# Experts' whole blocks: gate and up weights held in TensorE, turned rows streamed

## The reference, cut to what matters

```python
def _swiglu(combined):
    gate, up = jnp.split(combined, 2, axis=-1)
    return jax.nn.silu(gate) * up
...
combined = jnp.einsum('td,efd->tef', xf, expert_gate_up)   # d = 512, f = 2 * 512
hidden = _swiglu(combined)
expert_out = jnp.einsum('tef,edf->ted', hidden, expert_down)
sel_out = jnp.take_along_axis(expert_out, sel[:, :, None], axis=1)
routed_out = jnp.einsum('tk,tkd->td', gating, sel_out)
```

## Time and profile before

| | us |
|---|---|
| median of 3 runs | 1439.57 |
| lowest, highest | 1436.03, 1440.11 |
| span of the profiled execution | 1442.9 |
| TensorE busy in it | 1308.7 (91%) |
| VectorE, ScalarE, GpSimd busy | 583.3, 467.2, 200.8 |

### The profile page before, as it was taken

The page is one execution under the profiler, slowest core; times in us unless marked ns, Lnnn a source line. Parts: engine busy times, 40 slices in busy tenths (PEclk is TensorE's granted clock), DMA queues, the critical chain, the costliest instruction groups (busy, mean ns, idle before and its releaser), DMA issues.

```text
span 1442.9 us, 18224 instructions
## 1 busy us (share of the span) xinstructions
PE 1308.7 (91%) x5770; PEld 831.9 (58%) x5771; DVE 583.3 (40%) x1559; ACT 467.2 (32%) x1004; POOL 200.8 (14%) x207
## 2 busy tenths in 40 slices
PE   4899999999999899899898998988669999999798
PEld 3554485566466454377565775665445567565365
DVE  9999732111243351111111111111175333685894
ACT  5899632122122200011111111111113233227884
POOL 1000000000000055010100111101263000022370
PEclk8999999999999899999999999999879989999899
DMA  9100000000101214231246115253462000100001
GB/s 223 55 1 1 2 1 1 1 1 1 77 31 32 95 50 129 97 126 49 94 150 216 44 44 195 66 199 95 164 177 100 1 30 1 67 0 1 1 23 51
DMA packets 40976, 97.06 MB, mean 67 GB/s; under 512 B 4205, under 2 KB 6567, under 8 KB 39745
## 3 DMA queue, kind: packets, MB, share of 16 engines
q1 hardware_dynamic: 27205, 68.70, 14.3%
q0 software_dynamic: 6240, 16.39, 4.2%
q10 hardware_dynamic: 7452, 10.97, 2.1%
HBM read 79.91 MB, written 16.10 MB: 67 GB/s over the span
## 4 chain that ended last, share of the span: by engine, by line
PE 75%; DVE 11%; DMA 4%; issue 3%; ACT 3%; ACTq 1%; DVEq 1%; another core or an unknown queue 1%; POOL 0%; POOLq 0%
PE psum L433 38%; PE psum L1813 13%; PE psum L1868 7%; PE psum L1793 4%; DMA slot_outs<-sb_blk 3%; PE psum L2008 3%; PE psum L461 2%; DVE sb_hT_conv L1408 1%; PE psum L1951 1%; PE psum L1893 1%; PE psum L1925 1%; ACT sb_htok L807 1%; DMA sb_blk<-rows,sb_blk 1%; PE psum L1843 1%; DVE sb_blk L1201 1%
## 5 line engine op out<-in xcount | busy, mean ns | idle before, releaser
L433 PE MATMUL psum<-sb_w_reg,sb_blk 128*128 128x256 f32 x896 | 207.3, 385 | 1.2 <-issue 1.2
L433 PEld LDWEIGHTS psum<-sb_w_reg,sb_blk 128*128 128x128 f32 x896 | 170.1, 193 | 33.7 <-issue 12.4
L1813 PE MATMUL psum<-sb_z_reg_r,sb_hT_conv_r 125*125 125x512 f32 x400 | 170.9, 427 | 0.2 <-issue 0.2
L433 PE MATMUL psum<-sb_w_reg,sb_hT_conv 128*125 128x512 f32 (+1 forms) x376 | 168.6, 598 | 0.0
L1813 PE MATMUL psum<-sb_htok_r,sb_hT_conv_r 125*125 125x512 f32 x300 | 118.8, 396 | 0.0
L433 PE MATMUL psum<-sb_hT_conv,sb_w_reg 128*128 128x416 f32 (+3 forms) x336 | 108.2, 481 | 8.1 <-ACT sb_hT_conv L467 8.1
L1198 DVE TENSOR_TENSOR sb_blk<-sb_blk,psum 128x256 f32<-128x256 f32 x56 | 23.6, 421 | 227.4 <-ACT sb_blk L781 227.4
L433 PEld LDWEIGHTS psum<-sb_w_reg,sb_hT_conv 128*125 128x125 f32 (+1 forms) x376 | 68.6, 188 | 76.9 <-issue 76.3
L1868 PE MATMUL psum<-sb_w_reg,sb_blk 128*128 128x512 f32 x224 | 109.2, 610 | 2.2
L760 ACT CAST sb_hT_conv_r<-sb_a_reg 125x625 fp32r<-125x625 f32 x80 | 56.1, 715 | 116.6 <-PE psum L1813 116.5
L433 PEld LDWEIGHTS psum<-sb_hT_conv,sb_w_reg 128*128 128x128 f32 x336 | 67.2, 204 | 44.4 <-issue 40.3
(11 more groups left out here) (388 smaller groups left out, 1815.7 us busy)
## 6 DMA issues: line engine op xcount, KB each, us to landing
sb_hT_conv<-w_expert SPq DMA_DIRECT2D x7, 2048.0 KB, 12.5
sb_w_reg<-w_expert SPq DMA_DIRECT2D x6, 2048.0 KB, 10.6
sb_hT_conv<-w_expert SPq DMA_DIRECT2D x7, 1024.0 KB
slot_outs<-sb_blk ACTq DMA_DIRECT2D x28, 256.0 KB
sb_w_reg<-w_expert SPq DMA_DIRECT2D x6, 1024.0 KB, 12.6
sb_w_reg<-w_gnn SPq DMA_DIRECT2D x1, 4096.0 KB, 43.8
sb_w_reg<-w_qkv SPq DMA_DIRECT2D x1, 3072.0 KB, 20.5
slot_outs<-sb_blk ACTq DMA_DIRECT2D x1, 2560.0 KB, 10.5
```

The costliest lines, as they stand in the source:

```text
L433: ins = e.matmul(out, l, r, start=(n == 0), stop=(n == len(pairs) - 1))
L1813: ins = e.matmul(psum[0:TP, b, :], counts_at(l, 2 * i + n // NT)[:, s % HALF_T, :], z[s], start=(n == 0), stop=(n == len(pairs) - 1))
```

## The change

Gate and up of a whole block are computed the other way round. A piece of 128 features by 128 inner columns of the weights stands still, and the 128 turned rows of `xgT` stream. What lands in PSUM is the inner rows already turned, in the order in which `hidT` has them: for each half two pieces of gate side by side in columns 0 to 255 and two of up in 256 to 511. So 32 matmuls (64 passes) of 128 columns take the place of 16 (32 passes) of 256. VectorE's product goes straight to `hidT`; `pe_turn_hidden` and the copy out of PSUM are gone. The turn of the next rows comes right after gate and up, ahead of the whole down projection. `vec_block` raises `s_hid` and `s_ht` by 2 after the products so that the units' counts still fit, and the wait for PSUM to be read is on `s_he`, in blocks and in units. Units are otherwise as they were.

```diff
         def vec_block(e, g):
             for h in range(2):
                 e.wait_ge(s_sil, g * 2 + h + 1)
-                e.tensor_tensor(hid[:, h * HF:(h + 1) * HF], silg[:, h, :], psum[:, 1 + h, HF:2 * HF],
-                                ALU.mult).then_inc(s_hid, 1)
-                e.wait_ge(s_ht, g * 2 + h + 1)
-                e.tensor_copy(hidT[:, 2 * h:2 * h + 2, :].rearrange("p k n -> p (k n)"),
-                              psum[:, 3 + h, 0:256]).then_inc(s_he, 1)
+                e.tensor_tensor(hidT[:, 2 * h:2 * h + 2, :].rearrange("p k n -> p (k n)"), silg[:, h, :],
+                                psum[:, 1 + h, HF:2 * HF], ALU.mult).then_inc(s_he, 1)
+            e.sem_inc(s_hid, 2)
+            e.sem_inc(s_ht, 2)
...
         def pe_block(e, slot, landing, g):
             w_gu, w_dn = expert_views(slot)
             e.wait_ge(ld_up[slot], landing)
             e.wait_ge(s_xe, g + 1)
-            e.wait_ge(s_hid, g * 2 + 2)
+            e.wait_ge(s_he, g * 2 + 2)
             for h in range(2):
                 for part in range(2):
-                    if h == 1 and part == 1:
-                        pe_turn_hidden(e, g, 0)
-                    c = part * D_FF + h * HF
-                    ins = group(e, psum[:, 1 + h, part * HF:(part + 1) * HF],
-                                [(xgT[:, k, :], w_gu[:, k, c:c + HF]) for k in range(KD)])
+                    for f in range(2):
+                        c = part * D_FF + h * HF + f * 128
+                        ins = group(e, psum[:, 1 + h, part * HF + f * 128:part * HF + (f + 1) * 128],
+                                    [(w_gu[:, k, c:c + 128], xgT[:, k, :]) for k in range(KD)])
                 ins.then_inc(s_gu, 1)
+            pe_turn_rows(e, g + 1)
             e.wait_ge(ld_down[slot], landing)
             e.wait_ge(s_y, g + 1)
             for k in range(KD):
-                if k == 2:
-                    pe_turn_hidden(e, g, 1)
-                    pe_turn_rows(e, g + 1)
                 if k % 2 == 0:
                     e.wait_ge(s_he, g * 2 + k // 2 + 3)
                 ins = e.matmul(psum[:, 5, :], hidT[:, k, :], w_dn[:, k, :], start=(k == 0), stop=(k == KD - 1))
```

More of the change, by code:

```diff
@@ L1836, in pe_turn_rows @@
             ins.then_inc(s_xt, 1)
[L1838 to L1845, removed]
         def pe_block(e, slot, landing, g):
```

## The result

| | median us | lowest, highest | ratio to before, 95% interval |
|---|---|---|---|
| before | 1437.80 | 1433.90, 1440.11 | |
| after | 1414.87 | 1410.04, 1417.23 | 0.9844 [0.9817, 0.9872] |
| after, second series | 1414.40 | 1411.54, 1417.72 | 0.9841 [0.9807, 0.9875] |
| after, third series | 1413.40 | 1410.47, 1419.88 | 0.9823 [0.9800, 0.9846] |

What follows compares the result with a forecast made beforehand. TensorE's own instructions were taken to bound the steady block. 13.2 us from 24 steady blocks plus 13.4 from four first blocks, less 1.7 of clock, made 24.9: 1439.6 to 1414.7 us, range 1405 to 1426.

Steps and rivals of the forecast that it cites:

- The pace of gate and up: Gate and up of each block: 64 passes at 0.1115 us, 7.14 us in all, 0.24 more than before.
- The rival of a partly hidden load: Every gate and up pass: load and stream overlap only partly, 0.054 us more each, 96 us, 1511 us; chance 0.07.
- The steady block: A whole block in the experts' stage, TensorE never waiting: from 11.58 to 11.02 us, 0.55 taken as gain.
- the stall: Middle of down before: 0.24 us for VectorE's copy of the turned second half plus 0.10 bare weight load; 0.34 us goes.
- The 24 other blocks: Blocks of the experts' stage other than first blocks of turns: all steady, 24 x 0.55 = 13.2 us gained.
- The four first blocks: First blocks of turns, where TensorE waited 6.7 us for VectorE's product: 59.37 to 45.95 us, gain 13.4.
- The clock: Half-speed stretches after waits in the second and third first blocks vanish: 3.4 us gained, half of it counted.
- The moved row turn: Row turns go from the middle of down to its front: still 0.44 us, covering the second product, nothing gained.
- The waits at risk: Possible new waits for gather, products or output copies: taken as 0, except 0.17 us left in the fourth first block.
- The output copy's wait: After a turn's start, a late output landing could hold ScalarE: under 1 us in each of four turns, taken as 0.
- The longer loop body: Rival: TensorE's body of 152 instructions is fetched anew, some 2 us in each of 13 turns, about 1440 us; chance 0.03.
- The sum: Whole kernel: 13.2 + 13.4 = 26.6 us, less 1.7 for clock, 24.9 us off 1439.6, giving 1414.7 us.

Runs made afterwards that it cites:

- after, second series: The changed kernel run again unaltered, as the yardstick for follow-up experiments on the same chip: 1414.40 us.
- after, third series: The changed kernel run again unaltered with more rounds, as the yardstick for two repeated experiments: 1413.40 us.

## Why the prediction was right, point by point

**The pace of gate and up: right, 0.1116 for 0.1115 us.** The two rows of 65 and 2 columns carried it, and halving load and stream showed by trial that the load is the slower side. The rival of a partly hidden load, which the Trainium skill's 81 ns for a pair of 128 columns would have supported ("TensorE: Matmul & The Clock Gate", "Back-to-back issue gap"), does not hold here for fp32: 64 full streams behind 64 full loads run at the pace of the load alone. That settles the point which no row of before could decide. One figure of the working stands in no row, the stream of 0.213 us for 256 columns; the rows have 0.2157 for a pass, and the conclusion is the same with it.

**The steady block: right, 11.02 us.** Its gain splits as worked out: 10.78 us without the swap, so 0.24 us for the swap, and 11.56 - 10.78 = 0.78 us for the four turns and the stall. Nothing in it waits for either product.

**The 24 other blocks: 24 x (11.56 - 11.02) would be 13.0 us, but they gained 11.1, 13.1 and 11.1 us in the three profiles.** The prediction called all 24 steady. One is not: the first turn's first block took 11.67 us before and 13.15, 11.12 and 13.15 after, since in two profiles a half-speed stretch of the clock that began among the units ran on into it.

**The four first blocks: right in their main reason, with luck in the size.** Predicted 13.4 us; measured 14.7, 13.1 and 13.5 us in three profiles (59.37 less 44.66, 46.3 and 45.9). The 6.7 us of waiting are gone, 2.2 us are the shorter block (4 x 0.54), and the rest is mostly half speed, below. That the wait's place matters is shown by putting it back, but this returned only 6.0 and 4.0 us of these blocks and 4.6 and 5.5 of the medians. The part between, some 5 and 7 us, left with the outputs that land earlier in the block and with the clock; neither was tried by itself.

**The clock: a term that was mis-read.** I counted half of 3.4 us as gained. In the stage of before the clock stood at half speed in five stretches of 3.4 us; in the three profiles of after they sum to as much or one more: 17.1, 17.1 and 20.5 us. What changed is what they fall on. Three of the five lay in first blocks, one at a block's start and two right behind the waits for the product, and cost 5.1 us. After, half speed cost the four first blocks 0, 2.0 and 1.4 us, and the first turn's first block 2.1, 0 and 2.1. The other stretches lie among units, where TensorE waits for others anyway. So all blocks together gained 3.0, 3.2 and 1.5 us by the clock, without less half-speed time in the stage. That the sum came out within 1 us is in part luck of where these stretches fall.

**The moved row turn: a gain that I missed.** I priced it at nothing, by its own instructions and its cover in the block, and that was right there. But a row turn also releases the gather of the rows behind, and in the units that is late. The units took 1.8 and 3.4 us less than with the turn in the middle of down, in the two pairs of profiles. The units as a whole then took 98.0, 98.8 and 97.6 us against 99.4 before: an outcome near zero, made of a gain of 2 to 3 us by the move and a loss of about 1.4 us without it (100.6 and 101.0 against 99.4), for which I have no cause that a run singled out.

**The waits at risk: right.** Down waited for a product only in the fourth first block, 0.12 us where I had 0.17 (923.46 - 922.91 = 0.55 for turns of 0.43). The gather was never late in a block. The output copy's wait came, 3.87 us long, and stayed hidden, as estimated. The longer loop body cost nothing: five instruction packets in the stage, and blocks of 11.02 us in the middle of every turn.

**The sum.** Predicted for the stage 26.6 us with the clock's part; measured 27.2, 26.8 and 26.4 (436.5 less 409.3, 409.7 and 410.1). In the first profile that is 14.7 in the four blocks, 11.1 in the 24 others and 1.4 in the units. The medians moved less: the forecast was 24.9 us, and the three series gave 22.9, 22.7 and 22.9. The forecast time was met within 0.2 us also because the median of the kernel before stood at 1437.80 us in this comparison, where the prediction had started from 1439.57. Of the 4 us between the stage's gain and the medians' I can say only that all stage differences rest on the one long profile of before.

## What to carry to other kernels

When two operand orders stream the same number of columns, the order that delivers the result already turned may cost only the difference between load pace and stream pace: here 0.24 us a block, for 0.78 us of turns and waiting saved. The price could be read beforehand from loads of the same form with shorter streams. Ask of each wait that a change takes away where in the stage the waited-for engine is late for reasons of its own: four blocks with such a wait gained 13 to 15 us, about as much as the 24 others together. But put the wait back by itself before giving it the whole of that gain: it returned 4 to 6 us. And price a moved instruction by all that its semaphore releases, not by its own time: the same four turns at the front, in the middle or at the end of down gave 1413 to 1415, 1416 to 1420 and 1443 us.

## What the runs showed of the hardware

Fp32 weight loads of 128 columns hide whole under matmuls that stream 128 columns: 64 of each take 7.15 us, 0.1116 us a pair, where a load alone has that pace (0.111 with half the stream) and a stream alone 0.109 (with loads of 64 columns).

A weight load of another width than its neighbours was not free: with 64-column loads in gate and up between 128-column loads elsewhere, the pace fell to 0.109 us and the block still grew by 0.13 us, in gaps of 0.05 to 0.10 us at the changes. The width of what is written changed with it, so the cause may be either.

TensorE's clock can stay at its lower level through work without a pause. With half the stream, the stage's first block took 18.68 us, TensorE busy all the time; a steady block of the same kernel stands below it for comparison (columns as before, the clock is the third number from the end):

```profile
615.03:631.00 15.97, 15.97 (x76) 15.23 (x71) 0.84 (x2) 1.62 (x4) 0.18 (x1) 0.50 0.69 219
633.71:644.68 10.97, 10.97 (x78) 9.06 (x76) 0.84 (x2) 1.94 (x4) 1.15 (x2) 1.00 0.11 36
```

The clock had fallen to 1.2 GHz at 610.5, among the units, while TensorE waited 3.14 us for gathered rows, and came back only at 631.0, after the down projection with its 512-column streams had begun at 629.59. In the changed kernel's first profile, with full streams, the same first block holds half-speed time only from its start at 610.5 to 614.8, and takes 13.15 us. At full clock the same half streams did not make it fall. It is one run, and I ran nothing that tells why.
